# Two heads at a time: bias and running minimum of a head pair interleaved on VectorE, their logits in a row on TensorE, every stage's place in the order drawn anew

## The reference

```
# 1: attention to learned rows, 4 heads of 64 channels, 1024 rows
s = layernorm(x)*g + b;  p = square(relu(s_head @ k.T));  out = x + p @ v
# 2: cross attention, 16 heads of 16 channels, 256 keys per batch
logits = (Q @ K.T) * scale
D = clip(frac[:, None, :] - frac[:, :, None], -0.2, 0.2)
attn = gamma*logits + delta*(alpha_pos[h]*max(D, 0) + alpha_neg[h]*min(D, 0))
out = softmax(attn) @ V;  out = out @ Wo.T + bo
# 3: feed-forward 256 -> 1024 -> 256 with relu; the gate's top expert
#    adds a rank 4 correction lora_B[e] @ (lora_A[e] @ x) inside the relu
```

## Time and profile before

| | |
|---|---|
| time, median of 3 runs | 875.0 us (874.97 to 875.61) |
| profiled execution, span from first to last instruction | 873.6 us |
| TensorE busy | 851.8 us (98%), 7168 matmuls, granted clock 1.00 |
| VectorE busy | 756.6 us (87%), 2164 instructions |
| ScalarE busy | 711.7 us (81%), 1946 |
| GpSimd busy | 588.1 us (67%), 758 |

### The profile page before, as it was taken

One profiled execution on the slowest core, in us unless ns is written; L12 is line 12 of the kernel. 1 busy time (PEld: TensorE's weight loads), 2 busy tenths in 40 slices (PEclk: granted clock), 3 DMA queues, 4 the chain that ended last, 5 costly groups with the idle time before them and its releaser, 6 DMA issues.

```text
span 873.6 us, 20940 instructions
## 1 busy us (share of the span) xinstructions
PE 851.8 (98%) x7168; PEld 683.9 (78%) x7168; DVE 756.6 (87%) x2164; ACT 711.7 (81%) x1946; POOL 588.1 (67%) x758
## 2 busy tenths in 40 slices
PE   7999899999999999999999999999999999999997
PEld 6667578778778777877878787787878778788786
DVE  6888898889898898989889898988989888799964
ACT  5559898798888979888897888889888888879851
POOL 6758886768677776867777676677777677654421
PEclk9999999999999999999999999999999999999999
DMA  7223312212231221322222132222223122222200
GB/s 190 80 50 68 69 36 56 50 21 55 59 65 36 56 56 26 68 46 60 42 56 55 26 67 43 58 48 52 49 35 68 37 61 51 38 50 44 49 14 25
DMA packets 40187, 46.15 MB, mean 53 GB/s; under 512 B 10417, under 2 KB 27313, under 8 KB 40082
## 3 DMA queue, kind: packets, MB, share of 16 engines
q1 hardware_dynamic: 40082, 44.82, 25.2%
HBM read 15.42 MB, written 4.19 MB: 22 GB/s over the span
## 4 chain that ended last, share of the span: by engine, by line
PE 89%; ACT 4%; DVE 2%; SPq 2%; issue 1%; DMA 1%; POOL 0%; POOLq 0%; DVEq 0%
PE bank L300 12%; PE bank L404 12%; PE bank L253 10%; PE bank L485 10%; PE bank L417 7%; PE bank L395 7%; PE bank L288 7%; PE bank L289 6%; PE bank L373 3%; PE bank L495 2%; PE bank L354 2%; PE bank L334 2%; PE bank L379 2%; ACT P L701 1%; PE bank L320 1%
## 5 line engine op out<-in xcount | busy, mean ns | idle before, releaser
L1168 POOL TENSOR_SCALAR U<-DP,alph 128x512 f32<-128x512 f32 x256 | 192.3, 752 | 122.8 <-DVE NM L924 67.8
L701 ACT ACTIVATE P<-T,NM 128x256 f32<-128x256 f32 x512 | 256.3, 511 | 1.4 <-DVE NM L924 1.3
L1150 POOL TENSOR_TENSOR R<-R 128x512 f32<-128x512 f32 x208 | 219.2, 1054 | 44.8 <-ACT R L645 44.7
L917 DVE SCALAR_TENSOR_TENSOR bank<-DN,alph,bank 128x512 f32<-128x512 f32 x256 | 191.2, 747 | 28.5 <-PE bank L395 24.9
L924 DVE CUSTOM_DVE_ANT_0 T<-bank,U 128x256 f32<-128x256 f32 x512 | 197.0, 422 | 8.9
L621 ACT ACTIVATE STG<-bank 128x512 f32<-128x512 f32 x256 | 152.3, 595 | 38.4 <-PE bank L404 37.3
L645 ACT ACTIVATE R<-bank 128x512 f32<-128x512 f32 x248 | 146.8, 596 | 29.0 <-PE bank L289 24.4
L404 PE MATMUL bank<-ident,P 128*128 128x128 f32 x1024 | 155.6, 274 | 6.1 <-ACT STG L621 5.5
L404 PEld LDWEIGHTS bank<-ident,P 128*128 128x128 f32 x1024 | 118.3, 140 | 30.7 <-ACT P L701 14.7
L300 PE MATMUL bank<-R,VS 128*32 128x512 f32 x992 | 118.3, 593 | 0.6 <-issue 0.4
L395 PE MATMUL bank<-QS 128*128 128x256 f32 x512 | 111.8, 300 | 2.7 <-DVE NM L924 2.2
(11 more groups left out here) (184 smaller groups left out, 1886.4 us busy)
## 6 DMA issues: line engine op xcount, KB each, us to landing
QS<-QK SPq DMA_DIRECT2D x384, 64.0 KB, 2.4
XG<-in_x SPq DMA_DIRECT2D x16, 256.0 KB, 3.0
CT<-in_ctxT SPq DMA_DIRECT2D x16, 256.0 KB, 4.4
out<-XO SPq DMA_DIRECT2D x15, 256.0 KB, 2.2
FK<-in_frac SPq DMA_DIRECT2D x16, 128.0 KB, 3.3
STG<-in_wiT SPq DMA_DIRECT2D x2, 512.0 KB, 4.3
STG<-in_woT SPq DMA_DIRECT2D x2, 512.0 KB, 3.9
STG<-in_kT SPq DMA_DIRECT2D x2, 256.0 KB, 4.5
```

The lines of the kernel that those rows point to most:

```text
L701: eng.activation(P[n % NP][:, cs], T[n % NT][:, cs], ACT.Exp, bias=NM[:, n % 8, q:q + 1], scale=-1.0, accum_out=SU[n // 16 % 2][:, q, seat ...
L917: eng.scalar_tensor_tensor(out=L[:, :], in0=dn[:, :], scalar=alph[:, 16 + h:17 + h], in1=L[:, :], op0=ALU.mult, op1=ALU.add).then_inc(s_t1, 1)
L1150: eng.tensor_tensor(r, r, r, ALU.mult).then_inc(s_sqp, 1)
L1168: eng.tensor_scalar(U[n % NU][:, :], dp[:, :], alph[:, h:h + 1], 0.0, ALU.mult, ALU.add).then_inc(s_u, 1)
```

## The change

`biased` takes a pair of heads. It waits once for both heads' logits, issues the two bias operations (line 917) one behind the other, and then the four halves of the minimum (line 924). On TensorE the two heads' `logits` stand in a row, once per pair. No instruction on data is added or taken away.

```
-                for b, u in due(g, -7, 16, 39, early=4, late=7):
-                    logits(16 * b + u)
+                for b, u in due(g, -5, 8, 79, early=2, late=-1):
+                    logits(16 * b + 2 * u)
+                    logits(16 * b + 2 * u + 1)
...
-            def biased(n):
-                h, u, t, L = head(n), U[n % NU], T[n % NT], pL[n % 2]
-                dve.wait_ge(s_lg, n + 1)
-                dve.wait_ge(s_dn, n // 16 + 1)
-                eng.scalar_tensor_tensor(out=L[:, :], in0=dn[:, :], scalar=alph[:, 16 + h:17 + h],
-                                         in1=L[:, :], op0=ALU.mult, op1=ALU.add).then_inc(s_t1, 1)
-                dve.wait_ge(s_t1, n + 1)
-                dve.wait_ge(s_u, n + 1)
-                dve.wait_ge(s_ex, 2 * (n - 2))
-                for q in range(2):
-                    cs = slice(q * 256, q * 256 + 256)
-                    eng.tensor_tensor_reduce(out=t[:, cs], in0=L[:, cs], in1=u[:, cs], scale=-1.0, scalar=BIG,
-                                             op0=ALU.add, op1=ALU.min,
-                                             accum_out=NM[:, n % 8, q:q + 1]).then_inc(s_tt, 1)
+            def biased(p):
+                pair = (2 * p, 2 * p + 1)
+                dve.wait_ge(s_lg, 2 * p + 2)
+                dve.wait_ge(s_dn, p // 8 + 1)
+                for n in pair:
+                    h, L = head(n), pL[n % 2]
+                    eng.scalar_tensor_tensor(out=L[:, :], in0=dn[:, :], scalar=alph[:, 16 + h:17 + h],
+                                             in1=L[:, :], op0=ALU.mult, op1=ALU.add).then_inc(s_t1, 1)
+                for n in pair:
+                    u, t, L = U[n % NU], T[n % NT], pL[n % 2]
+                    dve.wait_ge(s_t1, n + 1)
+                    dve.wait_ge(s_u, n + 1)
+                    dve.wait_ge(s_ex, 2 * (n - 2))
+                    for q in range(2):
+                        cs = slice(q * 256, q * 256 + 256)
+                        eng.tensor_tensor_reduce(out=t[:, cs], in0=L[:, cs], in1=u[:, cs], scale=-1.0, scalar=BIG,
+                                                 op0=ALU.add, op1=ALU.min,
+                                                 accum_out=NM[:, n % 8, q:q + 1]).then_inc(s_tt, 1)
...
-                for b, u in due(g, 8, 16, 39, early=6, late=-5):
-                    biased(16 * b + u)
+                for b, u in due(g, 17, 8, 76, early=16, late=14):
+                    biased(8 * b + u)
```

On TensorE, the last transposes of X2 and block 3's second product:

```
-                for b, u in due(g, 1468, 8, 19, early=2, late=900):
+                for b, u in due(g, 1463, 8, 22, early=-32, late=910):
                     ffn_out(b, u)
...
-                for b, _ in due(g, 1093, early=36, late=-46):
+                for b, _ in due(g, 1109, early=-2, late=-148):
                     turned_over("x2T", b, X2, s_x2, 2 * b + 2, s_x2T)
```

On ScalarE and then VectorE:

```
-                if g == -930:
+                if g == -803:
                     act.wait_ge(s_wqs, 1)
                     weight("q", W["q"][0][:, :, :], view(512, 0, 128, 2))
...
-                if g == -290:
+                if g == -186:
                     weight("wb", IH[0:1, 0:2, :], view(1024, 2, 1, 2))
...
-                for b, _ in due(g, 7, early=-382, late=-6):
+                for b, _ in due(g, -73, early=-78, late=31):
                     differences(b)
...
-                if g == -348:
+                if g == -338:
                     centred("b", 0, X1, XG[0], s_x1)
...
-                for b, _ in due(g, 1195, early=-7, late=212):
+                for b, _ in due(g, 1196, early=8, late=87):
                     gating(b)
```

On GpSimd, one of the memsets that `restack` waits for, and on SyncE three loads:

```
-                if g == -946:
+                if g == -254:
                     pool.wait_ge(s_x0, 2)
                     eng.memset(f(QS[0][:, 0, :, :]), 0.0).then_inc(s_qz, 1)
...
-                if g == -1123:
+                if g == -2726:
                     load_c(0)
...
-                if g == -1034:
+                if g == -924:
                     sp.wait_ge(s_wlo["kT"], 2)
                     staged("q", 512, 128, 2, col(a["WqT"]))
-                if g == -495:
+                if g == -1303:
                     sp.wait_ge(s_wlo["v"], 1)
                     staged("o", 512, 128, 2, col(a["WoT"]))
```

More of the change, by code:

```diff
@@ L202, in due @@
                     yield NB - 1, u
-        GRID = range(-5 * PERIOD, (NB + 6) * PERIOD)
+        GRID = range(-8 * PERIOD, (NB + 8) * PERIOD)
         ring, used, bank_of = [0, 1, 2], {}, {}
@@ L592, in _ @@
                     turned_over("x1T", b, X1, s_x1, 2 * b + 2, s_x1T)
-                for b, _ in due(g, -241, early=-788, late=51):
+                for b, _ in due(g, -242, early=-691, late=24):
                     kp(b)
-                for b, _ in due(g, -213, early=43, late=-18):
+                for b, _ in due(g, -210, early=-32, late=34):
                     qp(b)
-                for b, _ in due(g, -142, early=70, late=4):
+                for b, _ in due(g, -122, early=49, late=-11):
@@ L604, in _ @@
                     gsT(b)
-                for b, _ in due(g, 1264, early=1, late=436):
+                for b, _ in due(g, 1274, early=10, late=414):
                     uT(b)
-                for b, u in due(g, -1161, 16, 37, early=-95, late=1):
+                for b, u in due(g, -1161, 16, 37, early=-12):
                     scores(b, u)
-                if g == -1784:
+                if g == -1971:
                     xnT(0)
-                if g == -688:
+                if g == -648:
@@ L612, in _ @@
                     xnT(1)
-                for b, _ in due(g, -1221, start=2, late=1):
+                for b, _ in due(g, -1234, start=2, late=-5):
                     xnT(b)
@@ L763, in _ @@
                     skh(0)
-                if g == -578:
+                if g == -675:
                     skh(1)
-                for b, _ in due(g, -1221, start=2, late=13):
+                for b, _ in due(g, -1204, start=2, late=-17):
                     skh(b)
-                for b, _ in due(g, -476, early=3, late=2):
+                for b, _ in due(g, -463, early=-13, late=10):
                     heads_out(b)
-                for b, u in due(g, 133, 16, 40, early=1, late=12):
+                for b, u in due(g, 148, 16, 40, early=-1, late=13):
@@ L817, in _ @@
                     gs(b)
-                for b, _ in due(g, 1278, early=-25, late=624):
+                for b, _ in due(g, 1295, early=-2, late=842):
                     ulh(b)
-                for b, u in due(g, -1137, 16, 36, early=20):
+                for b, u in due(g, -1122, 16, 36, early=-35, late=-2):
                     relu(b, u)
@@ L1115, in _ @@
                     ull(b)
-                for b, u in due(g, -1134, 16, 37, early=-109, late=27):
+                for b, u in due(g, -1064, 16, 33, early=-238, late=-8):
                     if on_dve(b, u):
@@ L1221, in _ @@
                     plus(X1b[b % 2], X1, boB, s_x1b)
-                for b, _ in due(g, 1405, early=178, late=258):
+                for b, _ in due(g, 1630, early=-93, late=-6):
                     pool.wait_ge(s_x2, 2 * b + 2)
@@ L1227, in _ @@
                     plus(X2b, X2, woB, s_x2b)
-                for b, u in due(g, -1076, 16, 37, early=101, late=-30):
+                for b, u in due(g, -1064, 16, 38, early=-362, late=18):
                     if not on_dve(b, u):
```

254 lines of the change are left out of this document (127 added, 127 removed).

## The result

The changed kernel takes 885.4 us (median of 4 runs, 884.1 to 886.3) against 875.3 us (4 runs) of the kernel before on the same chip: a ratio of 1.0108 (1.0087 to 1.0128). It is slower by 1.1%, where 872.0 us and a range of 866.5 to 878.0 were predicted. Its profiled execution has a span of 882.3 us, 8.7 more than before.

What follows compares the result with a forecast made beforehand. TensorE was taken as the bound, full from 150 to 750 us, with idle time at both ends. From a span of 873.6 us, -3.7 (head), +1.3 (order), -0.7 (tail) gave 870.5, plus 1.4 made 871.9, say 872; range 866.5 to 878.

Steps and rivals of the forecast that it cites:

- steps b and c: Middle batches: the pair's latency up to the gating and uT, taken as 0, and TensorE's new order, +1.3 us.
- It just fits, by 0.1 to 0.2 us. I take 0 for it: Last pair and gating: gating ends at 6.03 us, uT stands at 6.19; bounds 0 and 0.5 us a batch.
- rival A: Middle: VectorE late at the pair stalls uT or the next logits, 0.5 us a batch, 878.4 us; chance 0.26.
- Step (c): TensorE's order in the middle: one more switch behind transposes, +0.1 us a batch in 13 batches, +1.3 us.
- step d: Head: first logits 5.5 us earlier, less 1.8 us for fillers: -3.7 us, between -8 and +2.
- Four waits: Before the first logits: low context -1.5, wi_b -3.6, differences(0) -2.1, Wq +1.7 us; first logits at about 54.
- the step on Wq: Head: Wq issued behind Wo and taken after 10 relus instead of 6, +1.7 us, from 0 to 3.2 more.
- eight fillers at +1.8: Head: eight more fillers behind the first logits, where TensorE has little idle time, 0.23 us each, +1.8 us.
- step e: Tail: last batch's x2T before the last ffn_out step, whose matmuls cover its wait, -0.7 us, between -3 and +2.
- a head of -8: Lower bound of the head's estimate: all fillers hidden and Wq in time.
- step a: VectorE's interleaved pair: 2.72 us instead of 2.96, 1.9 us a batch less on VectorE, worth nothing by itself.
- Rival C: VectorE: second bias starts only when the first ends, pair takes 2.92 us, +2.6 at most, 874.5 us; chance 0.07.

Runs made afterwards that it cites:

- e1: The changed kernel with GpSimd's gain moved behind positive(15) instead of in front of it: 881.8 us, ratio 1.0060.
- e16: The kernel before with the context's first load behind the start's five loads and differences(0) behind Q's low part: 877.0 us, ratio 1.0004.
- e6: The changed kernel without the 22 fillers behind the first logits: 886.3 us, ratio 1.0115.
- e7: The kernel before without the 14 fillers behind its first logits: 876.8 us, ratio 1.0017.
- e11: The kernel before with the pair's logits and bias at the first head's place: 890.5 us, ratio 1.0166.
- e15: The kernel before with the pair at the first head's place, plus more fillers in batch 0's idle places on TensorE: 889.1 us, ratio 1.0142.

## Why the prediction was wrong

**The middle (steps b and c), +7.8 us where +1.3 stood.** The step that failed is "It just fits, by 0.1 to 0.2 us. I take 0 for it". Most of what it was made of was right (0.68 from logits to bias, 2.72 for the pair: 2.70 in e1, `gsT` 2.65 behind the logits). Three things were not. It took U to be there: the gating started 0.32 us late. It copied the gating's 2.63 us from the old order: it took 0.16 more. And it let `uT` start at the very end of the gating: it starts 0.14 later. Less the slack of 0.16, that is 0.46. Against rival A I had put that "GpSimd and ScalarE get heads no later than needed, by 3 us, in the order as sorted": GpSimd's queue was taken as a whole and not walked at this one place, where `gain`'s 2.6 us stood. Rival A, "a wait for VectorE in every batch" of 0.5 us at `uT`, is what happened: 0.46, in ten batches. It had 0.26. Even its 878.4 us is 7 us short of the measured time.

Step (c) was mis-sized: +0.1 us a batch was forecast and +0.29 measured. Its price of 0.09 us for a switch behind transposes is no cost: what the next block loses at its second matmul it gained by starting 0.08 us earlier behind the last transpose. What it left out is that a block moved nearer to its producer waits for it: the three short waits come to about 0.3 us.

**The head (step d), +0.4 us where -3.7 stood.** Four waits were taken as standing in a row, and their removals added. First logits came 1.6 us earlier (57.98), not 5.5. The waits for the context and `wi_b` are gone, yet ScalarE took Wqh at 25.88 us (18.21 before), where the step on Wq had +1.7, and VectorE was busy for 17.85 of the 20 us from 20 to 40 (15.80 before). e16 shows that two of the four, alone, are worth nothing in time (and its own edit made a new wait of 3.5 us); that VectorE is the next bound of the head rests on its busy time and the chain, not on a run of its own. The other term, eight fillers at +1.8, is borne out by no run: taking the fillers of this stretch out made neither kernel faster (e6, e7). The 0.4 us is then batch 0's own stretch, 85.0 us against 83.1.

**The tail (step e), +0.5 us where -0.7 stood**, within its bounds, and about +1.7 in the executions where the clock falls. x2T was moved; what outweighed it was not tested. The rest of the 13.5 us between 872 and 885.4 is that the median lies 3.1 us above the profiled span, where 1.4 was added. And the lower end of the range does not follow from its sum: a head of -8 gives 867.6, not 866.5.

**The pair itself (step a)** was right: 2.70 us, and worth nothing by itself. Rival C is refuted: two biases take 1.41 us together, one 0.75, so the second starts 0.66 behind the first. This is against the first half of what the Trainium skill says in "VectorE: DVE Perf Modes", section "The DRAIN you can't avoid", but the section itself adds that a next operation that is not held starts earlier, and that is what these rows show. "Busy time of VectorE about as before" was wrong: 741.0 us against 756.6, of which the biases give 11.3 (191.2 to 179.9) and the halves 9.4 (197.0 to 187.6), while other operations took some 5 more: the overlap of two neighbours is counted once in the busy time too.

## What to carry to other kernels

Where a new step "just fits", walk the queue of every engine that feeds it, at that one place and in the new order; a slack of 0.15 us is a bet, not a fit, and here 0.14 of it was the hand-over. A list of waits with a threshold hides short ones that come in every batch: compare the blocks from start to start. Waits in a head don't add up: price the removal of each by what is late next. Two operations joined must stand where the first one stood, and what was spaced for single ones, above all at the two ends, moves with them.

## What the runs showed of the hardware

A small VectorE operation of 0.17 us with both inputs in SBUF is held while GpSimd runs one: line 970 (`g`, `dec`) took 1.05 us up to 452.61, GpSimd's line 1158 ended at 452.57; in e1 line 975 (`g`, `gm`) ended at 451.17 and line 1158 at 451.14. Line 966, from PSUM, kept its 0.17 us. The Trainium skill says so in "SBUF — State Buffer", section "SBUF: two separate sides": the port pair that the two engines share is a lock held for a whole instruction. So the length of the gating, 2.13 to 2.79 us in the middle and 1.3 in the changed kernel's last three batches, where no operation of it was held, depends on what GpSimd does beside it, and a duration copied from one profile is not fixed.

The clock of a head with short idle stretches is not the same in every execution: the same instructions had 1.00 between 20 and 40 us in e11 and 0.91 in e15, with first logits at 59.44 and 61.85 us.
